# Four layers of graph convolution on one core: the relation passes with twice the slots, selection buffers and PSUM quads, and their dense step a turn later

## The chip, the cores and the metric

One Trainium2 chip, one of its cores. The metric is the device time of one launch in microseconds, median of several runs. The kernel before takes 6027.67 us.

## The reference

`x` has 5000 nodes of 128 features and there are 80000 edges, sorted by destination. Four layers follow one another, each `x = x + layer(relu(layernorm(x)))`: attention over edges, a weighted sum over edges, three averaging convolutions, and three relational convolutions. The last is what this change touches. Each of its convolutions is

```
seg  = dst * 8 + etype
agg  = segment_sum(x[src], seg)            # per node and relation
mean = agg / max(count, 1)
out  = einsum('nrd,rdo->no', mean, W) + x @ root + b
```

with widths 128 to 256, 256 to 256 and 256 to 128, and a relu after the first two.

## The kernel before, in words

**Order of the products.** The kernel multiplies before it gathers. For every node it makes the 8 products with the relations' matrices and stores them as 8 rows of a table in DRAM (`tab_l3a`, `tab_l3b`, `tab_l3c`, 40960 rows of 256, 256 and 128 floats). An edge then needs the one row of its source and its relation, divided by the edge count (`WGT`), and the sum over the edges of a node is the convolution. So there are three relation passes, numbered 5, 6 and 7 in the code (`sums(5, ...)` and so on), each with 80000 / 128 = 625 tiles of 128 edges. Pass 0, in an earlier layer, has the same form.

**A pass.** POOL gathers a tile by one indirect DMA (line 945, `gather`) into one of 16 slots of `ring`. Four tiles are a quad, and four quads, 16 tiles, are a turn; there are 157 quads and 39 turns. For each quad DVE makes a selection matrix in two instructions (lines 1776 and 1778, `select`): where an edge's destination falls in a window of 64 nodes, times the weight. PE multiplies each tile's rows by it and adds up the four tiles in a PSUM bank (line 2365, `tile`), and DVE adds the quad to the accumulator in SBUF at the window's place (line 1789, `quad`), one of `ACC_A` and `ACC_B`, features by nodes.

**What paces it.** Semaphores alone. `mm_done` counts quads that PE has finished: POOL waits for it before it refills the slots of the quad four before, DVE before it adds. `s_ready` counts selections, `psum_free` counts adds. DVE selects two quads ahead (`AHEAD`), in four buffers of `QSEL`; PE uses PSUM banks 0 to 3, one quad each, and may write a quad when the one four before has been added. The credits are at lines 2360 and 2361:

```
pe.wait_ge(sem("s_ready"), kr * (QUADS + AHEAD) + g + 1)
pe.wait_ge(sem("psum_free"), kq + g + 1)
```

**The dense step.** Beside pass 5 the table of pass 6 is made and beside pass 6 that of pass 7, a block of 128 nodes in each turn. The function `turns` says which block's steps stand in which turn and `dense_step` puts the 16 steps between the 16 tiles: tiles 0 to 3 of turn i carry the last four steps of block i - 2, tiles 4 to 15 the first twelve of block i - 1. There are 40 blocks, and two whole ones are left after the last turn (`remaining`). Step 0: ACT waits for the quad just added and makes the relu of the block's columns (line 1306, `hidden`) into `part_hid`, two buffers. Step 2: PE waits for it and multiplies by the root matrix (line 2396) into bank 5. Step 3: ACT adds the bias and stores it to the other accumulator, where the next pass starts (line 1102). Steps 4, 7, 10, 13: PE makes a unit, 512 columns of the block's table rows (line 2406), in banks 6 and 7 by turns; pass 6 has steps 4 and 7 alone. Two steps after each, ACT copies the bank to `unit_rows` (line 1112), and PE waits for the copy before it writes this bank again. SP stores a block's rows to the table (line 836, `store_units`). Pass 7 has no table to make: ACT copies a block (line 1330), PE transposes it into bank 4 or 5 (line 2669), DVE adds `x` (line 2217) and SP stores the result (line 855).

**Between passes.** POOL starts the gathers of a pass when the table is stored, DVE when all root products are in the accumulator.

## Time and profile before

| what | value |
|---|---|
| median of 3 runs | 6027.67 us (6023.32 to 6033.74) |
| profiled execution, first to last instruction | 6607.7 us |
| its own time beside the span | not given by the page; at least the span |
| PE, DVE, ACT, POOL busy in it | 4440, 2724, 1078, 4114 us |
| mean granted TensorE clock | 0.718 of full |
| relation passes | 3784.7 to the end |

The profile is one execution while every instruction is recorded. Its times are microseconds from its first instruction. Engines are PE (TensorE), PEld (its weight loads), DVE (VectorE), ACT (ScalarE), POOL (GpSimd) and SP. An fp32 matmul stands as two records. In a row of waits the engine and line are the ones that waited; "issue" is a time in which nothing that the profile knows held the engine, "remote" one that ended by a signal for which it found no recorded work that had just ended.

### The profile page before, as it was taken

The numbers are of one execution on the slowest core, as the hardware profiler recorded it, in microseconds if no ns is written. First come the engines' busy times: TensorE is split into PE (matmuls) and PEld (weight loads), VectorE is DVE, ScalarE is ACT, GpSimd is POOL, SyncE is SP. The second block draws the span as 40 slices with busy tenths as digits, with TensorE's granted clock in tenths as the row PEclk, the third lists the DMA queues.
The fourth block names the chain that finished last, engine by engine and source line by source line (L and its number), as shares of the span: only waits on it lengthen the run. The fifth ranks groups of instructions, "written<-read, shape, count | busy, mean of one in ns | idle before, by whom it ended". The sixth has DMA issues, their size and how long they took to land.

```text
span 6607.7 us, 91944 instructions
## 1 busy us (share of the span) xinstructions
PE 4440.1 (67%) x24058; PEld 3442.2 (52%) x24058; DVE 2723.9 (41%) x8965; ACT 1077.6 (16%) x2081; POOL 4113.5 (62%) x3656
## 2 busy tenths in 40 slices
PE   2456676666666665999989977777766776533333
PEld 1344555544444444988876655555555555433333
DVE  7965555677777774322236411111111111111112
ACT  2521111122222222111113311111100000000000
POOL 2356666488888885744445466666566666566666
PEclk6566666666666666999999977888867666655555
DMA  6622222256555555744457734444333333211111
GB/s 158 210 71 77 76 77 76 67 100 102 99 98 100 99 100 153 221 146 131 125 177 255 255 121 132 133 130 133 122 109 114 110 111 109 75 52 50 52 50 50
DMA packets 569636, 764.26 MB, mean 116 GB/s; under 512 B 87625, under 2 KB 468064, under 8 KB 558608
## 3 DMA queue, kind: packets, MB, share of 16 engines
q1 hardware_dynamic: 327884, 422.38, 20.1%
q0 software_dynamic: 190256, 287.00, 20.1%
q10 hardware_dynamic: 51334, 52.94, 2.4%
q8 instruction: 75, 1.23, 0.1%
q14 instruction: 87, 0.71, 0.0%
HBM read 526.51 MB, written 235.79 MB: 115 GB/s over the span
## 4 chain that ended last, share of the span: by engine, by line
PE 32%; issue 17%; another core or an unknown queue 16%; DVE 11%; DMA 10%; POOL 9%; DVEq 3%; ACT 1%; ACTq 0%; POOLq 0%; SPq 0%
PE PS L2495 10%; DMA part<-ring,cur 8%; PE PS L2365 7%; POOL ring L945 5%; PE PS L2406 5%; POOL part L967 3%; DVE ACC_B L1755 2%; PE PS L2632 2%; PE PS L2396 2%; PE PS L2330 1%; DVE ACC_B L1753 1%; DVE QSEL L1776 1%; PE PS L2427 1%; PE PS L2572 1%
## 5 line engine op out<-in xcount | busy, mean ns | idle before, releaser
L2365 PE MATMUL PS<-QSEL,ring 128*128 128x64 f32 x7436 | 1393.7, 339 | 723.0 <-issue 327.9
L2365 PEld LDWEIGHTS PS<-QSEL,ring 128*128 128x128 f32 x7436 | 1354.3, 257 | 937.1 <-issue 671.3
L967 POOL DMA_INDIRECT part<-ring,cur x625 | 1010.0, 1616 | 250.9 <-issue 154.3
L945 POOL DMA_INDIRECT ring<-tab_l3b,SRC x625 | 599.7, 959 | 357.5 <-issue 208.6
L945 POOL DMA_INDIRECT ring<-tab_l3a,SRC x625 | 596.7, 955 | 359.0 <-issue 197.8
L945 POOL DMA_INDIRECT ring<-tab_l,SRC x593 | 587.9, 991 | 360.7 <-issue 160.8
L945 POOL DMA_INDIRECT ring<-tab_l3c,SRC x625 | 598.4, 957 | 326.0 <-issue 202.4
L2330 PE MATMUL PS<-ACC_B 128*128 128x320 f16 x2568 | 622.5, 410 | 116.2 <-issue 60.7
L1789 DVE TENSOR_TENSOR ACC_B<-ACC_B,PS 128x128 f32 (+1 forms) x314 | 79.7, 254 | 1429.1 <-remote 1006.6
L2406 PE MATMUL PS<-XM,SCR 128*128 128x512 f32 x960 | 580.7, 737 | 28.6 <-issue 14.5
L2427 PE MATMUL PS<-SCR,SEL 128*32 128x128 f32 x1250 | 275.2, 402 | 418.4 <-DVE SCR L1825 334.8
L1755 DVE TENSOR_SCALAR ACC_B<-ACC_B 128x640 f16<-128x640 f16 x1284 | 498.4, 450 | 0.0
L2330 PEld LDWEIGHTS PS<-ACC_B 128*128 128x128 f16 x2568 | 300.1, 127 | 359.0 <-issue 118.1
L2427 PEld LDWEIGHTS PS<-SCR,SEL 128*32 128x32 f32 x1250 | 188.7, 160 | 482.4 <-DVE SCR L1825 355.6
L1753 DVE TENSOR_SCALAR ACC_B<-ACC_B 128x128 f16<-128x128 f16 x1284 | 253.1, 287 | 339.2 <-PE PS L2330 257.9
L1789 DVE TENSOR_TENSOR ACC_A<-ACC_A,PS 128x64 f32 (+1 forms) x314 | 78.7, 251 | 726.7 <-remote 498.2
L1059 ACT CAST ACC_B<-PS 128x640 f16<-128x640 f32 x320 | 221.5, 692 | 586.7 <-PE PS L2330 334.0
L1112 ACT COPY SCR<-PS 128x512 f32<-128x512 f32 x240 | 138.2, 587 | 1095.8 <-remote 652.7
L2406 PEld LDWEIGHTS PS<-XM,SCR 128*128 128x128 f32 x960 | 204.1, 235 | 199.9 <-issue 182.2
L2040 DVE TENSOR_TENSOR SCR<-PS,ring 128x128 f32<-128x128 f32 (+1 forms) x120 | 40.2, 335 | 586.6 <-PE PS L2495 571.2
L2495 PE MATMUL PS<-ACC_exact,slots_exact 128*128 128x512 f32 x1070 | 263.8, 397 | 0.0
L1776 DVE TENSOR_TENSOR QSEL<-iotaQ,QREL 128x256 f32<-128x256 f32 x477 | 201.5, 422 | 87.2 <-issue 86.2
(494 smaller groups left out, 6767.0 us busy)
## 6 DMA issues: line engine op xcount, KB each, us to landing
ring<-pairs_d SPq DMA_DIRECT2D x60, 1280.0 KB
pairs_d<-ACC_B ACTq DMA_DIRECT2D x320, 160.0 KB
SCR<-pairs_d SPq DMA_DIRECT2D x40, 1280.0 KB
SCR<-in_src SPq DMA_DIRECT2D x128, 320.0 KB
tab_l3a<-SCR SPq DMA_DIRECT2D x40, 1024.0 KB, 4.4
tab_l3b<-SCR SPq DMA_DIRECT2D x40, 1024.0 KB
ACC_A<-pairs_d SPq DMA_DIRECT2D x20, 1280.0 KB
tab_l3c<-SCR SPq DMA_DIRECT2D x40, 512.0 KB
```

What stands on the lines that cost most here:

```text
L945: pool.indirect_dma_start(gathered(p, slot), None, tab[p][:, :], bass.IndirectOffsetOnAxis(SRC[:, t:t + 1], 0)).then_inc(sem(f"pair_in{slo ...
L967: pool.indirect_dma_start(part_d[m][:, :], bass.IndirectOffsetOnAxis(cur[:, s:s + 1], 0), ring[:, s, 0:D], None, compute_op=ALU.add).then_ ...
L1059: nc.scalar.copy(SPAN_OUT[:, v, :].rearrange("p (h c) -> p h c", h=2), PS[:, 6:8, 0:SPAN_COLS // 2]).then_inc(sem("span_out"), 1)
L1753: vec.tensor_scalar(LOWS[:, v, e, :], iota_low, LOW[:, bass.ds(tile + e, 1)], None, ALU.is_equal)
L1755: ins = vec.tensor_scalar(PAIRS[:, v, e, :], iota_pairs, KEY[:, bass.ds(tile + e, 1)], OFFS[:, bass.ds(at, 1)], ALU.subtract, ALU.is_equal)
L1776: vec.tensor_tensor(hot[:, s, :, :], there, at, ALU.is_equal).then_inc(sem("s_hot"), 1)
L1789: vec.tensor_tensor(v, v, PS[:, s, 0:C * QWIN].rearrange("p (c w) -> p c w", w=QWIN), ALU.add).then_inc(sem("psum_free"), 1)
L2330: ins = mm(PS[:, 6 + h, 0:SPAN_COLS // 2], LOWS[:, v, e, :], PAIRS[:, v, e, h * (SPAN_COLS // 2):(h + 1) * (SPAN_COLS // 2)], start=e == 0 ...
L2365: ins = mm(PS[:, s, ch * QWIN:(ch + 1) * QWIN], rows, hot, start=e == 0 and ch == 0, stop=e == end, skip_group_check=True)
L2406: ins = mm(PS[:, 6 + m % 2, :], part_hid[:, u, ch, :], relw[:, at:at + 512], start=ch == 0, stop=ch == kc - 1)
L2427: ins = mm(windows_out[0:WIN, j * P:(j + 1) * P], SEL[:, j, :], same[:, j, :], start=True, stop=True)
L2495: ins = mm(to if conv == 1 else to.rearrange("p (k n) -> p k n", k=2), slot[:, e * P:(e + 1) * P], conv_source(conv, h), start=h == 0, sto ...
```

## The change

- The three relation passes leave `turns`, `remaining` and `sums` for functions of their own (`deep_turns`, `deep_remaining`, `deep_sums`, and `deep_steps` on ACT). Pass 0 keeps the old ones, now cut to its case.
- The gather has 32 slots (`DEEP`): the 16 of `ring` and 16 in `MULTI`, a buffer that is free by then. POOL waits for the quad eight before, and a landing semaphore counts a quad, not a pair.
- Selections have 8 buffers (`SEL_BUFS`), four of them in `MULTI`, made in place, and DVE selects 6 quads ahead (`LEAD`).
- PSUM banks 0 to 3 hold two quads each. PE waits once for every pair of quads, and DVE waits for both before it adds the first.
- The dense step of a block stands one turn later (`DEEP_LAG`: tiles 0 to 3 carry block i - 3, tiles 4 to 15 block i - 2), so three whole blocks are left after the last turn. Its relu is made by DVE in the middle of the turn, after the first pair's adds, block i - 1 in turn i; PE uses it at tile 6 of turn i + 1. DVE waits there for the copies of the block two before.
- Units stand at steps 3, 5, 7 and 11 in banks 6, 7, 4 and 6, ACT's copies one step later, and one semaphore counts them.

The diff, cut to its core:

```diff
+DEEP = 2 * SLOTS
+SEL_BUFS = 8
+LEAD = 6
+DEEP_LAG = 3
...
+        def deep_turns(eng, turn):
+
+            turn(0, None, None, 0, 0)
+            turn(1, None, None, 1, 0)
+            turn(2, None, (0, 0, 0), 0, 1)
+            pairs = (TURNS - DEEP_LAG) // 2 - 1
+            with eng.Fori(0, pairs) as r:
+                turn(2 * r + DEEP_LAG, (2 * r, 0, r), (2 * r + 1, 1, r), 1, r + 1)
+                turn(2 * r + DEEP_LAG + 1, (2 * r + 1, 1, r), (2 * r + 2, 0, r + 1), 0, r + 2)
+            for b in range(2 * pairs, TURNS - DEEP_LAG):
+                turn(b + DEEP_LAG, (b, b % 2, b // 2), (b + 1, (b + 1) % 2, (b + 1) // 2), (b + DEEP_LAG) % 2, (b + DEEP_LAG) // 2)
...
-            return ring_flat[:, slot * D:(slot + 1) * D] if p == 0 else ring[:, slot, 0:PASS[p]["F"]]
+            if p == 0:
+                return ring_flat[:, slot * D:(slot + 1) * D]
+            if slot < SLOTS:
+                return ring[:, slot, 0:PASS[p]["F"]]
+            return MULTI[:, (slot - SLOTS) * HID:(slot - SLOTS) * HID + PASS[p]["F"]]
+
+        def chosen_by(s):
+
+            if s < 4:
+                return QSEL[:, s, :, :]
+            at = SLOTS * HID + (s - 4) * QUAD * QWIN
+            return MULTI[:, at:at + QUAD * QWIN].rearrange("p (e w) -> p e w", e=QUAD)
+
+        def deep_landings(quad):
+
+            return sum(t % DEEP // QUAD == quad for t in range(T))
+
+        def deep_sums_bank(s):
+
+            return s % SEL_BUFS // 2, s % 2 * HID
 
...
+        UNIT_BANK = (6, 7, 4, 6)
+        UNIT_STEPS = (3, 5, 7, 11)
...
-                slots, per = (FIRST_SLOTS, QUAD) if p == 0 else (SLOTS, 2)
+                slots, per = (FIRST_SLOTS, QUAD) if p == 0 else (DEEP, QUAD)
...
-            def hidden(p, acc, k, b, u, added):
-                act.wait_ge(sem("psum_free"), added)
-                nc.scalar.activation(part_hid[:, u, :, :], block_cols2(acc, b), ACT.Relu).then_inc(sem("hid_made"), 1)
-
             def t6_dense(j, k, b, u, r, added):
-                if j == 0:
-                    hidden(6, ACC_B, k, b, u, added)
                 if j == 3:
                     root_bias(ACC_A, 3, 2, nth_block(act, km, k, b, 0), b)
-                if j in (6, 9, 12, 15):
-                    unit_rows_out(6, (j - 6) // 3, k, b, u, r)
-            dense_steps(5, t6_dense)
+                if j - 1 in UNIT_STEPS:
+                    unit_rows_out(6, UNIT_STEPS.index(j - 1), k, b, u, r)
+            deep_steps(5, t6_dense)
...
+            def deep_sums(p, hidden, dense):
+                c = PASS[p]
+                acc, C = c["acc"], chunks(p)
+                rounds_reset(f"p{p}")
+                with dve.Fori(0, km) as k:
+                    kq = dve.snap((km * ORD[p] + k) * QUADS)
+                    hots = dve.snap(km * (QUADS + AHEAD) + (km * (ORD[p] - 1) + k) * QUADS)
+                    round_start(f"p{p}", k)
+                    if hidden is not None:
+                        dve.wait_ge(sem("unit_out"), nth_block(dve, km, k, 0, p - 5, TABLES[p + 1][1], 4) + 1)
+
+                    def select(g, s):
+                        if isinstance(g, int) and g >= QUADS:
+                            return
+                        there = iotaQ[:, :].unsqueeze(1).to_broadcast([P, QUAD, QWIN])
+                        at = cols(QREL, g, QUAD).unsqueeze(2).to_broadcast([P, QUAD, QWIN])
+                        hot = chosen_by(s % SEL_BUFS)
+                        vec.tensor_tensor(hot, there, at, ALU.is_equal).then_inc(sem("s_hot"), 1)
+                        dve.wait_ge(sem("s_hot"), hots + g + 1)
+                        vec.tensor_tensor(hot, hot, cols(c["wt"], g, QUAD).unsqueeze(2).to_broadcast([P, QUAD, QWIN]), ALU.mult) \
+                            .then_inc(sem("s_ready"), 1)
+
+                    def quad(g, s, first):
+                        bank, at = deep_sums_bank(s)
+                        dve.wait_ge(sem("psum_free"), kq + g + CREDIT)
+                        v = acc[:, 0:C, bass.ds(first, QWIN)]
+                        vec.tensor_tensor(v, v, PS[:, bank, at:at + C * QWIN].rearrange("p (c w) -> p c w", w=QWIN), ALU.add).then_inc(sem("psum_free"), 1)
+
+                    def pair(g, s, bases):
+                        select(g + LEAD, s + LEAD)
+                        dve.wait_ge(sem("mm_done"), kq + g + 3)
+                        quad(g, s, bases[0])
+                        select(g + LEAD + 1, s + LEAD + 1)
+                        quad(g + 1, s + 1, bases[1])
+
+                    def block_hidden(b, u, added):
+                        dve.wait_ge(sem("psum_free"), added)
+                        if not isinstance(b, int) or b >= 2:
+                            dve.wait_ge(sem("unit_out"), nth_block(dve, km, k, b, p - 5, TABLES[p + 1][1], 4) - TABLES[p + 1][1] + 1)
+                        vec.tensor_scalar(part_hid[:, u, :, :], block_cols2(acc, b), 0.0, None, ALU.max).then_inc(sem("hid_made"), 1)
+
+                    def turn(i, last, first, h, use):
+                        bases = windows(dve, regs[0:4], QBASE[0:1, bass.ds(4 * i, 4)], QWIN)
+                        for x in range(2):
+                            g = 4 * i + 2 * x
+                            pair(g, 4 * h + 2 * x, bases[2 * x:2 * x + 2])
+                            if hidden is not None and x == 0 and later(i):
+                                block_hidden(i - 1, 1 - h, dve.snap(kq + g + 2 + CREDIT))
+                            for j in range(8 * x, 8 * x + 8):
+                                dense_step(dense, j, k, last, first, None)
+                    for g in range(LEAD):
+                        select(g, g)
+                    deep_turns(dve, turn)
+                    bases = windows(dve, regs[0:4], QBASE[0:1, bass.ds(QUADS - 1, 4)], QWIN)
+                    dve.wait_ge(sem("mm_done"), kq + QUADS + 1)
+                    quad(QUADS - 1, (QUADS - 1) % SEL_BUFS, bases[0])
+                    added = dve.snap(kq + QUADS + CREDIT)
+                    dve.wait_ge(sem("psum_free"), added)
+                    dve.sem_inc(sem("turn"), 1)
+                    if hidden is not None:
+                        for b in range(TURNS - 1, BLOCKS):
+                            block_hidden(b, b % 2, added)
...
+            def deep_sums(p, dense):
+                C = chunks(p)
+                with pe.Fori(0, km) as k:
+                    kr = pe.snap(km * (ORD[p] - 1) + k)
+                    kq = pe.snap((km * ORD[p] + k) * QUADS)
+                    chosen_before = pe.snap(km * (QUADS + AHEAD) + kr * QUADS)
+                    pe.wait_ge(sem("psum_free"), kq + CREDIT)
+                    pe.sem_inc(sem("turn"), 1)
+
+                    def landed(quad, use):
+                        return km * (16 * first_landings(quad)) + kr * (16 * deep_landings(quad)) + use * (16 * QUAD) + 16 * QUAD
+
+                    def tile(g, s, e, slot, landed, end):
+                        bank, at = deep_sums_bank(s)
+                        if e == 0:
+                            pe.wait_ge(sem(f"pair_in{slot // QUAD}"), landed)
+                            pe.wait_ge(sem("s_ready"), chosen_before + g + 1)
+                            if s % 2 == 0 and (not isinstance(g, int) or g >= SEL_BUFS):
+                                pe.wait_ge(sem("psum_free"), kq + g + (CREDIT + 2 - SEL_BUFS))
+                        rows, hot = gathered(p, slot), chosen_by(s)[:, e, :]
+                        for ch in range(C):
+                            ins = mm(PS[:, bank, at + ch * QWIN:at + (ch + 1) * QWIN], rows[:, ch * P:(ch + 1) * P], hot,
+                                     start=e == 0 and ch == 0, stop=e == end, skip_group_check=True)
+                        if e == end:
+                            ins.then_inc(sem("mm_done"), 1)
+
+                    def turn(i, last, first, h, use):
+                        for j in range(TURN):
+                            slot = h * TURN + j
+                            tile(4 * i + j // QUAD, 4 * h + j // QUAD, j % QUAD, slot, landed(slot // QUAD, use) if j % QUAD == 0 else None, QUAD - 1)
+                            dense_step(dense, j, k, last, first, None)
+                    deep_turns(pe, turn)
+                    last = (T - 1) % DEEP
+                    tile(QUADS - 1, (QUADS - 1) % SEL_BUFS, 0, last, landed(last // QUAD, (T - 1) // DEEP) - 16 * (QUAD - 1), 0)
+                    deep_remaining(lambda j, b, u, r: dense(j, k, b, u, r, None))
...
-                emptied = nth_block(pe, km, k, b, p - 6, units // 2, 2)
-                pe.wait_ge(sem("unit_outd" if m % 2 else "unit_outa"), emptied + m // 2 + 1)
+                pe.wait_ge(sem("unit_out"), nth_block(pe, km, k, b, p - 6, units, 4) + (2 if m == 3 else 1))
                 for ch in range(kc):
                     at = (ch * units + m) * 512
-                    ins = mm(PS[:, 6 + m % 2, :], part_hid[:, u, ch, :], relw[:, at:at + 512], start=ch == 0, stop=ch == kc - 1)
+                    ins = mm(PS[:, UNIT_BANK[m], :], part_hid[:, u, ch, :], relw[:, at:at + 512], start=ch == 0, stop=ch == kc - 1)
...
-                if j in (4, 7, 10, 13):
-                    unit(6, (j - 4) // 3, k, b, u)
-            sums(5, t6_dense)
+                if j in UNIT_STEPS:
+                    unit(6, UNIT_STEPS.index(j), k, b, u)
+            deep_sums(5, t6_dense)
```

## Rows read from the trace of the kernel before

**Rows 1.** The page's first line: the profiled execution.
```profile
span 6607.7 us, 91944 instructions
```

**Rows 2.** Line 945, the gathers: ns min/median/max, first and last start in us.
```profile
L945 POOL DMA_INDIRECT ring<-tab_l3a,SRC x625: 943/949/1167, 3784.7 to 4714.8; - x157
L945 POOL DMA_INDIRECT ring<-tab_l3b,SRC x625: 943/949/1196, 4751.0 to 5672.0; - x157
L945 POOL DMA_INDIRECT ring<-tab_l3c,SRC x625: 942/947/1202, 5695.8 to 6596.3; - x157
```

**Rows 3.** Same view: POOL idle before gathers of all four passes: us, times.
```profile
  remote: 495.6, 174
  PE PS L2365: 82.2, 56
  PE PS L2367: 55.8, 14
```

**Rows 4.** POOL's waits in each relation pass: waited for, us, times, longest.
```profile
POOL ring L945 <- remote: 109.0, 39, 4.0
POOL ring L945 <- PE PS L2365: 52.2, 29, 4.3
...
POOL ring L945 <- remote: 120.2, 36, 4.6
POOL ring L945 <- PE PS L2365: 28.8, 23, 4.3
...
POOL ring L945 <- remote: 122.4, 37, 5.9
POOL ring L945 <- PE PS L2365: 1.2, 4, 0.3
```

**Rows 5.** Third relation pass, timeline: start us, us, what, idle before and its releaser.
```profile
6129.51 1.12 PE L2365 MATMUL PS<-QSEL,ring 128*128 128x64 f32 x4 [1.19 <-DMA ring<-tab_l3c,SRC]
...
6134.52 1.12 PE L2365 MATMUL PS<-QSEL,ring 128*128 128x64 f32 x4 [1.25 <-DMA ring<-tab_l3c,SRC]
...
6136.89 0.95 POOL L945 DMA_INDIRECT ring<-tab_l3c,SRC  x1 [0.31 <-issue]
...
6141.49 0.22 DVE L1789 TENSOR_TENSOR ACC_B<-ACC_B,PS 128x64 f32 x1 [16.45 <-remote]
6141.63 0.42 DVE L1776 TENSOR_TENSOR QSEL<-iotaQ,QREL 128x256 f32<-128x256 f32 x1
6142.07 0.95 POOL L945 DMA_INDIRECT ring<-tab_l3c,SRC  x1 [4.24 <-remote]
...
6142.52 0.22 DVE L1789 TENSOR_TENSOR ACC_B<-ACC_B,PS 128x64 f32 x1
```

**Rows 6.** POOL's waits in the scatter stretch, 1300 to 2500: the largest.
```profile
POOL part L967 <- issue: 149.7, 483, 0.6
```

**Rows 7.** Stretches: busy us of PE, PEld, DVE, ACT, POOL; PE clock, DMA, GB/s.
```profile
3784.00:4715.00 931.00, 721.76 (x3367) 524.06 (x3368) 161.33 (x459) 122.26 (x260) 595.97 (x625) 0.80 0.42 131
4751.00:5672.00 921.00, 636.06 (x2917) 517.41 (x2918) 160.95 (x462) 73.18 (x150) 598.73 (x625) 0.68 0.36 110
5695.00:6597.00 902.00, 332.93 (x1282) 287.74 (x1282) 163.57 (x496) 11.31 (x38) 598.08 (x625) 0.50 0.19 51
4715.00:4751.00 36.00, 26.22 (x95) 13.79 (x93) 6.47 (x20) 9.44 (x20) 0.77 (x1) 0.97 0.33 112
```

**Rows 8.** Timeline of the tails of the first and second relation pass.
```profile
4726.51 0.42 ACT L1306 ACTIVATE SCR<-ACC_B 128x256 f32<-128x256 f32 x1
...
4726.98 1.16 PE L2396 MATMUL PS<-SCR,root 128*128 128x128 f32 x8 [0.99 <-ACT SCR L1306]
...
4735.52 0.42 ACT L1306 ACTIVATE SCR<-ACC_B 128x256 f32<-128x256 f32 x1
...
5681.41 0.42 ACT L1306 ACTIVATE SCR<-ACC_A 128x256 f32<-128x256 f32 x1 [3.42 <-DVE ACC_A L1789]
...
5686.54 0.42 ACT L1306 ACTIVATE SCR<-ACC_A 128x256 f32<-128x256 f32 x1
```

More of the change, by code:

```diff
@@ L431, in dense_step, with deep_remaining @@
                 dense(j - SLACK, k, *first, added)
+        def deep_turns(eng, turn):
[8 more added lines that the diff above has]
+                turn(b + DEEP_LAG, (b, b % 2, b // 2), (b + 1, (b + 1) % 2, (b + 1) // 2), (b + DEEP_LAG) % 2, (b + DEEP_LAG) // 2)
+        def deep_remaining(step):
+            for b in range(TURNS - DEEP_LAG, BLOCKS):
+                for j in range(TURN - SLACK if b == TURNS - DEEP_LAG else 0, TURN):
+                    step(j, b, b % 2, b // 2)
         def remaining(step):
@@ L1083, in dense_steps, with deep_steps @@
                     remaining(lambda j, b, u, r: dense(j, k, b, u, r, added))
+            def deep_steps(p, dense):
+                with act.Fori(0, km) as k:
+                    kq = act.snap((km * ORD[p] + k) * QUADS)
+                    def turn(i, last, first, h, use):
+                        added = act.snap(kq + TURN // QUAD * (i - 1) + (CREDIT + SLACK // QUAD)) if first is not None else None
+                        for j in range(TURN):
+                            dense_step(dense, j, k, last, first, added)
+                    deep_turns(act, turn)
+                    added = act.snap(kq + QUADS + CREDIT)
+                    deep_remaining(lambda j, b, u, r: dense(j, k, b, u, r, added))
             def norm_root(n):
@@ L2373, in turn @@
                         for j in range(TURN):
-                            slot = u * TURN + j if p == 0 else j
-                            tile(4 * i + j // QUAD, j // QUAD, j % QUAD, slot, None if p == 0 and last is None else landed(slot, i if p else r), QUAD - 1,
-                                 TURN * i + j if p == 0 and last is None else None)
+                            slot = u * TURN + j
+                            tile(4 * i + j // QUAD, j // QUAD, j % QUAD, slot, None if last is None else landed(slot, r), QUAD - 1,
+                                 TURN * i + j if last is None else None)
                             dense_step(dense, j, k, last, first, added)
@@ L2387, in sums, with turn @@
                     added = pe.snap(kq + QUADS + CREDIT)
                     remaining(lambda j, b, u, r: dense(j, k, b, u, r, added))
+            def deep_sums(p, dense):
[11 more added lines that the diff above has]
+                        if e == 0:
+                            pe.wait_ge(sem(f"pair_in{slot // QUAD}"), landed)
+                            pe.wait_ge(sem("s_ready"), chosen_before + g + 1)
[7 more added lines that the diff above has]
+                            ins.then_inc(sem("mm_done"), 1)
+                    def turn(i, last, first, h, use):
+                        for j in range(TURN):
+                            slot = h * TURN + j
[4 more added lines that the diff above has]
+                    tile(QUADS - 1, (QUADS - 1) % SEL_BUFS, 0, last, landed(last // QUAD, (T - 1) // DEEP) - 16 * (QUAD - 1), 0)
+                    deep_remaining(lambda j, b, u, r: dense(j, k, b, u, r, None))
```

55 lines of the change are left out of this document (22 added, 33 removed).

## The prediction, made before the change was run

> **What bounds the kernel now.** I read the profile from the outside in: the span, the gathers of the three relation passes, what their engine waited for, one held stretch, PE's clock, and what follows a pass's last gather. The profiled execution spans 6607.7 us [rows 1]; the median of the runs is 6027.7, that is 580.0 less. This gap carries much of the forecast and comes back below.
>
> The relation passes take 625 gathers each, one after another on POOL: first start to last start 930.1, 920.9 and 900.6 us [rows 2]. A gather is busy for 0.95 us and the next follows 0.30 later [rows 5], so 625 that never wait need 625 x 1.25 = 781 us. The rest is waiting for a free slot: 109.0 + 52.2 = 161.2 us in the first of the passes, 120.2 + 28.8 = 149.0 in the second, 122.4 + 1.2 = 123.6 in the third, 433.8 together [rows 4]. Over all four gather passes the kinds of wait sum to 495.6 + 82.2 + 55.8 = 633.6 us [rows 3]. No other engine bounds them: PE is busy 721.8 of 931 us, 636.1 of 921 and 332.9 of 902, DVE 161 to 164 [rows 7].
>
> What releases these waits is PE's signal that a quad is done, and it comes late. In [rows 5] PE ends one quad at 6129.51 + 1.12 = 6130.63 and the next at 6135.64, 5.0 us apart. DVE, which needs only the signals, begins the adds of waiting quads at 6141.49 and 6142.52, 1.0 us apart, after 16.45 us of idleness that no recorded release explains ("remote"). POOL stopped after the gather of 6136.89 and went on at 6142.07, 4.24 us idle. The third pass has 37 such waits, longest 5.9 us [rows 4]: about one for each time that POOL goes round its 16 slots. In the scatter stretch, where POOL's largest wait is mere issue [rows 6], that view has no remote entry at all. So a signal held for up to 16 us meets a ring of 16 slots, which is 16 x 1.25 = 20 us deep, of which landing and PE's work already take a part.
>
> **The change part by part.** (a) *32 slots instead of 16.* A quad's slots are wanted again after eight quads, 40 us, not after four, 20 us. No gather is added. If a held signal comes through chiefly once POOL has gone quiet ([rows 5]: 3.6 us after POOL's last busy moment, 6136.89 + 0.95), the same pause of some 4 us is paid once per 32 gathers: the stall halves. If it comes through on its own in 16 us, the 40 us hide it and the stall goes. If it lasts as long as the ring, or is not a delay of the signal at all, nothing goes. I take the half: the pauses recur at the ring's period and the release seen came only in the quiet. Ends: nothing and all.
>
> (b) *Eight selection buffers, lead of six; eight quads in PSUM.* Before, PE may run two quads past what DVE has been told; it stops for s_ready or psum_free, which is why a deeper ring alone would be useless. The two selection instructions per quad (0.42 us each [rows 5]) are only issued earlier; DVE has 930 - 161 us of room. At a pass's start four more quads are selected ahead, 4 x 0.84 = 3.4 us, beside the first gathers' landing; only the first selection is awaited. Cost nothing. DVE adds quads in pairs, so every other add waits up to one quad (5 us), which the eight buffers cover; if they did not, PE would stop and (a) would be lost.
>
> (c) *Dense step a turn later, relu on DVE.* 40 relus in each of two passes leave ACT (0.42 us each [rows 8]) and stand in DVE's queue, between the adds; the nearest DVE instruction, the selection of the same 128x256, takes 0.42 too. 80 x 0.42 = 34 us on DVE, hidden by its idleness. Bounds: 0, or 34 if each stood before an add that POOL awaits; I take 0. DVE now also waits there for the copies of the block two before: queued behind it are the second half of the turn's adds and selections, but those copies precede the quads just added in PE's order. In exchange PE's root product at tile 6 no longer waits for a relu of the same turn.
>
> (d) *Three unit banks.* Unit products and their copies are as many as before, 160 and 80. The waits for a freed bank go from 6 tiles' distance to 8 (bank 6) or 16 (7 and 4). Bank 4 held the transposes of the last pass only, which still has it. SP's wait is merged, its stores are as many, POOL's landing semaphore now covers four gathers: PE starts a quad up to 2.5 us later, inside the 40. Nothing on the path; if PE did not have the room, see the third rival.
>
> (e) *The tail.* Blocks left after a pass's last quad: three whole ones instead of two. A block in the first tail takes 4735.52 - 4726.51 = 9.0 us, in the second 5686.54 - 5681.41 = 5.1 [rows 8]; in each, 0.99 us is PE idle for the relu, which DVE now makes ahead. First tail: +9.0 - 3 x 1 = +6; second: +5.1 - 3 = +2; in the last pass, a copy and a transposition more, +1. Together +9 us, all on the path, for POOL may not start the next pass before the table is stored. Bounds: 0, and 9.0 + 5.1 + 1 = 15.
>
> **The sum.** Against the profiled execution: -433.8 / 2 + 9 = -208, so a span near 6400. For the runs I need the share of the stall that they have. The stall of all gather passes, 633.6, is a little more than the whole excess of the profiled execution, 580.0. If all of the excess is stall that recording brings about, the runs keep 53.6 of 633.6, 8%, and the three passes have 37 us of it. If none is, they keep it all, scaled by 6027.7 / 6607.7 = 0.912: 396 us. No row divides the excess (91944 recorded instructions may each cost a little too), so I take half of it: 633.6 - 290 = 343.6, 54%, and 433.8 x 0.54 = 235 us in the three passes. Half of that goes: -118 + 9 = -109, and 6027.7 - 109 = 5919.
>
> **Rivals.** *1, nothing to be had.* Either the runs hardly stall: -18 + 9 = -9, 6018; or the hold lasts until POOL stops, and the pauses grow with the ring: +9, 6037. For it: how nearly 580 and 633.6 agree. Against: the waits are much alike in all three passes, whatever PE's load. Here stands also that PE is truly as late as its signals and its records stand too early. Against that, [rows 5]: DVE finds two quads done 1.0 us apart, of which each took PE two bursts of 1.1 us. The Trainium skill, "Perfetto Trace Analysis", section "Tensor Engine Instruction (MATMUL, LD_WEIGHTS)", says that a matmul's recorded end is estimated and that its semaphore is pushed only after PSUM has acknowledged. By that rule PE would be the true bound, a deeper ring would bring nothing, and the time would be 6037; DVE's starts disagree with it, at least in size.
>
> *2, the ring hides it all.* The hold is a delay of some 16 us and 40 us of slots cover it: -235 + 9 = -226, 5802; with all the stall in the runs -396 + 9, 5641. For it: DVE's idle of 16.45 us [rows 5] is well under 40. Against: the signal came only when POOL was quiet.
>
> *3, slower: PE in the first relation pass.* PE did 721.8 us of work at a granted clock of 0.80 [rows 7], 577 at full clock. It lies between the levels of 1.2 and 2.4 GHz; in the last pass, busy 333 of 902 us, it was 0.50, and in the first tail, nearly without gaps, 0.97. A hold that lasts 40 us leaves PE waiting for unit banks, then with eight quads and two blocks to make up at the low level. Below a mean clock of 577 / 931 = 0.62 PE becomes the bound of this pass. At 0.56, midway to the floor: 577 / 0.56 = 1031, +100, +91 in the runs; with +9 and half of the other two passes' stall, 272.6 x 0.54 / 2 = 74, gained: 6054. The second pass has 636.1 x 0.68 = 433 and could not become PE-bound above 0.47. Against it: the lead of six lets PE work through a hold that stops it today. The Trainium skill, "TensorE: Matmul & The Clock Gate", section "Why this matters for your kernels", warns that idle gaps between bursts send the clock back to its lower level; [rows 7] agree (0.50 with gaps, 0.97 without).
>
> **How the numbers follow.** A measurement of this kernel can tell 0.2%, 12 us, from no change. Forecast 0.40, rival 1 0.20, rival 2 0.22, rival 3 0.15, others 0.03. Faster: 0.40 + 0.22 and a little of rival 1, 0.66. Same 0.17, slower 0.17. The time is that of the likeliest, 5919. The range runs from 5720, between rival 2 and its extreme, to 6060, past rival 3: left out are a full hiding of a full stall and a PE slower than 0.56. The forecast's own range, from a quarter to three quarters of the excess, is 5870 to 5970.
>
> **What would show it.** Right: POOL's waits in the three passes about 217 us in place of 433.8, half as many; passes of some 850, 845 and 840 us; PE busy at a clock no lower than 0.75 in the first; relus on DVE at 0.4 us; the gap to the next pass 6 us longer. (a) is wrong if as many waits remain or each is twice as long; (b) if PE waits for selections; (d) if PE waits for unit copies; (e) if the tails do not grow. The split of the excess is wrong if the changed kernel's span falls by 200 and its runs by under 30, or by as much as the span. The forecast fails if the span falls by less than 100.

## The result, and the profile after

The changed kernel takes 6040.46 us, median of 11 runs (6039.15 to 6046.54). The kernel before, run beside it, takes 6029.61 (11 runs, 6023.32 to 6036.15). The ratio is 1.002, with a 95% interval of 1.0012 to 1.0028: slower by 0.2%, 10.9 us. The forecast was 5919.

The first view is the head of the changed kernel's page and its gathers, each pass now in two rows, one for the 16 slots in `ring` and one for the 16 in `MULTI` (`XM` in the trace). The columns are those of [rows 2].

```profile
span 6038.5 us, 91019 instructions
...
L985 POOL DMA_INDIRECT ring<-tab_l3a,SRC x320: 942/947/1194, 3601.3 to 4390.8; - x160
L985 POOL DMA_INDIRECT XM<-tab_l3a,SRC x305: 942/947/1182, 3621.8 to 4392.0; - x153
...
L985 POOL DMA_INDIRECT ring<-tab_l3b,SRC x320: 941/947/1192, 4431.4 to 5217.0; - x160
L985 POOL DMA_INDIRECT XM<-tab_l3b,SRC x305: 942/947/1193, 4451.8 to 5218.3; - x153
...
L985 POOL DMA_INDIRECT ring<-tab_l3c,SRC x320: 940/945/1199, 5240.4 to 6026.2; - x160
L985 POOL DMA_INDIRECT XM<-tab_l3c,SRC x305: 940/945/1187, 5260.3 to 6027.4; - x153
```

The passes, first start to last start, are 790.7, 786.9 and 787.1 us, against 930.1, 920.9 and 900.6 in [rows 2]. That looks like a gain of 387 us, yet the time did not fall. Note the span: 6038.5 here against 6607.7 in [rows 1], while the runs of the two kernels are 11 us apart. The two profiled executions are not alike in something other than the kernel. POOL's waits in the first and the second pass, as in [rows 4]:

```profile
POOL ring L985 <- issue: 120.3, 315, 24.6
POOL XM L985 <- issue: 91.1, 299, 0.3
POOL XM L985 <- PE PS L2516: 1.8, 6, 0.3
POOL ring L985 <- PE PS L2516: 1.5, 5, 0.3
...
POOL ring L985 <- issue: 133.2, 312, 38.4
POOL XM L985 <- issue: 90.8, 298, 0.3
POOL ring L985 <- PE PS L2516: 2.4, 8, 0.3
POOL XM L985 <- PE PS L2516: 2.1, 7, 0.3
```

What is left is the 0.30 us between one gather and the next. The waits put down to PE sum to 3.3 and 4.5 us, none of them longer than 0.3, and the third pass has none. Engines and clock by stretch, with the columns of [rows 7]:

```profile
3600.00:4393.00 793.00, 663.51 (x3349) 501.86 (x3350) 169.22 (x496) 108.34 (x219) 601.48 (x625) 0.84 0.48 153
4393.00:4431.00 38.00, 31.44 (x112) 16.93 (x110) 7.62 (x23) 10.68 (x21) 0.00 (x0) 0.97 0.35 126
4431.00:5219.00 788.00, 627.14 (x2914) 515.73 (x2915) 171.01 (x492) 56.43 (x110) 597.42 (x625) 0.68 0.43 129
...
5240.00:6029.00 789.00, 308.45 (x1278) 280.08 (x1278) 157.46 (x490) 11.01 (x37) 597.84 (x625) 0.50 0.22 58
```

Nothing of rival 3: PE's clock in the first pass is 0.84, and it works 31 of 38 us in the tail. So there were two questions: what does the kernel *before* look like in an execution like those that were timed, and where do 11 us come from?

### The profile page after: what moved, and what is told of

It reads as the page before. It is cut to its first block, busy times and chain, and to the rows that moved or that the text cites. A ratio compares the mean times of both kernels' runs of the same rounds, so it can differ in the third digit from the quotient of the medians.

```text
span 6038.5 us, 91019 instructions
## 1 busy us (share of the span) xinstructions
PE 4329.7 (72%) x24058; PEld 3381.9 (56%) x24058; DVE 2738.3 (45%) x9033; ACT 1049.6 (17%) x2001; POOL 4110.3 (68%) x3656
## 3 DMA queue, kind: packets, MB, share of 16 engines
q0 software_dynamic: 190256, 287.00, 22.1%
## 4 chain that ended last, share of the span: by engine, by line
POOL 38%; PE 23%; issue 16%; DMA 14%; DVE 6%; DVEq 1%; ACT 1%; POOLq 1%; SPq 0%; ACTq 0%
POOL ring L985 21%; POOL XM L985 13%; DMA part<-ring,cur 11%; PE PS L2635 11%; POOL part L1007 3%; PE PS L2516 2%; PE PS L2772 2%; PE PS L2546 2%; PE PS L2441 1%; PE PS L2712 1%; PE PS L2714 1%; PE PS L2725 1%; DVE ACC_B L1801 1%; DMA XM<-tab_l3b,SRC 0%; PE PS L2662 0%
## 5 line engine op out<-in xcount | busy, mean ns | idle before, releaser
L2516 PE MATMUL PS<-QSEL,ring 128*128 128x64 f32 x3200 | 570.1, 344 | 415.0 <-DMA ring<-tab_l3c,SRC 251.5
L2516 PEld LDWEIGHTS PS<-QSEL,ring 128*128 128x128 f32 x3200 | 549.4, 258 | 504.1 <-issue 463.5
L2516 PE MATMUL PS<-XM 128*128 128x64 f32 x3050 | 543.8, 344 | 372.4 <-DMA XM<-tab_l3c,SRC 229.8
L2516 PEld LDWEIGHTS PS<-XM 128*128 128x128 f32 x3050 | 523.8, 258 | 457.8 <-issue 419.3
L985 POOL DMA_INDIRECT ring<-tab_l3b,SRC x320 | 305.9, 956 | 135.6 <-issue 133.2
L985 POOL DMA_INDIRECT ring<-tab_l3a,SRC x320 | 308.2, 963 | 121.9 <-issue 120.3
L985 POOL DMA_INDIRECT ring<-tab_l3c,SRC x320 | 305.7, 955 | 118.4 <-issue 118.4
L985 POOL DMA_INDIRECT XM<-tab_l3a,SRC x305 | 293.3, 962 | 93.0 <-issue 91.1
L985 POOL DMA_INDIRECT XM<-tab_l3c,SRC x305 | 292.2, 958 | 93.0 <-issue 93.0
L985 POOL DMA_INDIRECT XM<-tab_l3b,SRC x305 | 291.7, 956 | 93.0 <-issue 90.8
L2473 PE MATMUL PS<-QSEL,ring 128*128 128x64 f32 x1186 | 261.2, 355 | 83.1 <-DMA ring<-tab_l,SRC 82.3
L2473 PEld LDWEIGHTS PS<-QSEL,ring 128*128 128x128 f32 x1186 | 245.7, 261 | 133.6 <-issue 118.5
```

The source lines that it names most:

```text
L985: pool.indirect_dma_start(gathered(p, slot), None, tab[p][:, :], bass.IndirectOffsetOnAxis(SRC[:, t:t + 1], 0)).then_inc(sem(f"pair_in{slo ...
L2473: ins = mm(PS[:, s, ch * QWIN:(ch + 1) * QWIN], rows, hot, start=e == 0 and ch == 0, stop=e == end, skip_group_check=True)
L2516: ins = mm(PS[:, bank, at + ch * QWIN:at + (ch + 1) * QWIN], rows[:, ch * P:(ch + 1) * P], hot, start=e == 0 and ch == 0, stop=e == end, s ...
```

## The experiments

Each table row below is one kernel: its time (median, lowest to highest, runs), the kernel before on the same chip, and the ratio with its interval. The stages come from one profile each: first to last gather of the three relation passes, then the two gaps (last gather of a pass to first of the next) and the end (last gather to the end of the span).

### The kernel before again, and 16 slots

`before_again` is the kernel before, unchanged. 

> The kernel before, unchanged, profiled once more. Theory T (tail): the late signals of PE belong to the first profiled execution and not to the kernel; here the span is within 10 us of the 6029.6 us of its runs, each relation pass takes 785 to 800 us from first to last gather, POOL's waits other than issue are under 30 us in all three passes, and the gap from the last gather of one pass to the first of the next is 31 to 37 and 18 to 24 us. Rival S (stall): the kernel before really stalls and the change gave the gain back elsewhere; here the passes take 840 us or more and POOL waits 40 us or more in each.

Its gathers, and POOL's waits put down to PE in the three passes:

```profile
L945 POOL DMA_INDIRECT ring<-tab_l3a,SRC x625: 942/946/1197, 3597.9 to 4384.0; - x157
...
L945 POOL DMA_INDIRECT ring<-tab_l3b,SRC x625: 942/946/1197, 4417.4 to 5207.2; - x157
...
L945 POOL DMA_INDIRECT ring<-tab_l3c,SRC x625: 940/944/1163, 5231.6 to 6014.3; - x157
```

```profile
POOL ring L945 <- PE PS L2365: 16.7, 55, 0.3
...
POOL ring L945 <- PE PS L2365: 9.1, 30, 0.3
...
POOL ring L945 <- PE PS L2365: 19.5, 64, 0.3
```

This settles the larger question. The same kernel, recorded in the same way, now spans 6022.2 us and takes 6023.9, so recording costs nothing that is seen here. With 16 slots its passes are 786.1, 789.8 and 782.8 us: as short as with 32. No wait is longer than 0.3 us, which is the usual distance between two gathers under another name. There is no stall to remove.

`slots16` is the changed kernel with its ring put back to 16 slots, all else kept:

```diff
-DEEP = 2 * SLOTS
+DEEP = SLOTS
...
-                            slot = h * TURN + j
-                            tile(4 * i + j // QUAD, 4 * h + j // QUAD, j % QUAD, slot, landed(slot // QUAD, use) if j % QUAD == 0 else None, QUAD - 1)
+                            slot = j
+                            tile(4 * i + j // QUAD, 4 * h + j // QUAD, j % QUAD, slot, landed(slot // QUAD, 2 * use + h) if j % QUAD == 0 else None, QUAD - 1)
```

> The changed kernel with 16 slots again, all else of it kept (selection lead, eight quads in PSUM, late dense step, relu on DVE, banks). Theory T: POOL has nothing to wait for with 16 slots either, so 6040 us, within 6 of the changed kernel. Rival S: the ring is what keeps POOL going, so the passes lengthen by 40 us each and the time is above 6100.

### The tail: a lag of two turns, and the changed kernel again

`lag2` keeps the ring, the buffers, the banks and the relu on DVE, but moves the dense step a turn forward again. The root product then stands at tile 6 of the turn in which the relu is made, and the units at 7, 8, 10 and 14.

```diff
-DEEP_LAG = 3
+DEEP_LAG = 2
...
-        UNIT_STEPS = (3, 5, 7, 11)
+        UNIT_STEPS = (7, 8, 10, 14)
...
```

> The changed kernel with the dense step as early as before (two whole blocks left after the last quad, not three), its root product and units at later tiles of the turn because DVE makes the relu after a pair of quads. Theory T: the third block is what the change added to the path, 7.8 us in the first tail, about 4 in the second and 1 in the last: 6040.5 - 13 = 6027, at or a little under the kernel before. Rival S: the tail is not what costs; the time stays at 6040 or rises, because PE again waits for the relu of the same turn.

`after_again` is the changed kernel once more, for a second profile. 

> The changed kernel, unchanged, profiled once more, to see whether late signals of PE turn up in a profile of it. Theory T: a span within 10 us of 6040 as in its first profile, no such signals; if they do turn up, they are a matter of the execution. Rival S: the same, so this run tells only of how far one profile can be trusted.

| kernel (chip 0; before 6029.33, 21 runs) | time | ratio | passes | gaps, end |
|---|---|---|---|---|
| before_again | 6023.92, one | | 786.1, 789.8, 782.8 | 33.4, 24.4, 7.9 |
| slots16 | 6041.23 (6031.92 to 6043.96, 11) | 1.002 [1.0011, 1.0029] | 786.6, 785.8, 784.1 | 40.5, 25.0, 11.0 |
| lag2 | 6037.51 (6034.58 to 6043.75, 11) | 1.0017 [1.0008, 1.0026] | 788.4, 787.8, 787.7 | 35.1, 25.4, 8.9 |
| after_again | 6034.17, one | | 787.5, 785.6, 784.1 | 39.6, 22.4, 11.1 |

Going back to 16 slots changes neither time nor passes: the ring is worth nothing here, and costs nothing. The gaps and the end sum to 65.7 us in the kernel before, to 72.6 in the first profile of the changed one (39.4 + 22.1 + 11.1) and to 73.1 in the second. `lag2` brings the sum to 69.4, but was expected at 6027 and came to 6037.5: 3 us of the 13 hoped for. The end of its first pass, and the first product of a whole block after it:

```profile
4388.70 0.95 POOL L984 DMA_INDIRECT XM<-tab_l3a,SRC  x1 [0.30 <-issue]
4390.07 0.58 ACT L1165 COPY SCR<-PS 128x512 f32<-128x512 f32 x1 [1.54 <-PE PS L2545]
...
4401.07 1.16 PE L2536 MATMUL PS<-SCR,root 128*128 128x128 f32 x8
4401.20 0.58 ACT L1165 COPY SCR<-PS 128x512 f32<-128x512 f32 x1 [2.02 <-PE PS L2545]
```

Four copies of an earlier block's units, from 4390.07 to 4401.20, stand behind the last gather, and the first root product of a whole block comes 12.4 us after it. The changed kernel has four such copies too, but its root product follows after 8.8 (4400.84 - 4392.03 in its first profile). From that product to the first gather of the next pass `lag2` takes 22.7 us and the changed kernel 30.6. So the third block costs the 7.8 us that were expected of it, and 3.6 of them are lost again in the stretch before the whole blocks. That the later steps of `lag2` do this is likely but not shown, as this stretch varies by itself: it is 11.7 us in `after_third`. Its second gap, 25.4, is longer than the changed kernel's 22.1.

### One part each, on a chip that behaves like the first profile

The next four ran on another chip. `before_third` is the kernel before. 

> The kernel before, unchanged, profiled a third time. Theory T: as in its second profile, span 6015 to 6035, passes of 783 to 790 us, gaps of about 33.4 and 24.4 us, 8 us at the end, first relation gather near 3598 us (if it is nearer 3602, as in both profiles of the changed kernel, the part ahead of the relation passes adds nothing to the difference). Rival R (rare state): a span above 6500 with late signals of PE again.

`late_only` is the kernel before with the dense step of passes 5 to 7 a turn later and nothing else: the order of turns and of what remains is that of the change, and ACT's relu awaits the adds of the turn before.

```diff
...
-                        added = act.snap(kq + TURN // QUAD * i + (CREDIT + SLACK // QUAD))
+                        added = act.snap(kq + TURN // QUAD * (i if p == 0 else max(i - 1, 0) if isinstance(i, int) else i - 1) + (CREDIT + SLACK // QUAD))
...
-                    turns(act, turn)
+                    (late_turns if p else turns)(act, turn)
```

> The kernel before with one part of the change, the dense step a turn later in the three relation passes; relu on ScalarE, 16 slots, two unit banks as before. Theory T: a whole block more in each tail at the price of before, 9.0 and 5.1 us and 1 to 3 at the end: gaps of 42 and 29.5 us, 6029.3 + 16 = 6045 us, slower than the changed kernel, whose relu made ahead gives part of it back. Rival P (the passes): the tail is paid for by fewer waits inside the passes and the time stays at 6029.

`lead2` is the changed kernel with DVE selecting two quads ahead, as before, in place of six.

```diff
-LEAD = 6
+LEAD = 2
```

> The changed kernel with selections made 2 quads ahead instead of 6. Theory T: POOL is never held by PE, so the lead is worth nothing, 6040 us within 6, or 1 to 3 us less at each pass start, where fewer selections are made first. Rival P: the lead keeps PE from stopping, and without it the passes lengthen and the time rises above 6050.

`relu_ahead` is the kernel before with nothing changed but the relu, made by DVE after the turn's first quad.

```diff
-                if j == 0:
-                    hidden(6, ACC_B, k, b, u, added)
...
+                            if relu and g == 0 and first is not None:
+                                block_hidden(first[0], first[1], added)
```

> The kernel before with one other part of the change, the relu on VectorE, here right after the turn's first quad; dense step no later, 16 slots, two unit banks. Theory T: in the tails PE no longer waits 0.99 us for the second block's relu and little less for the first: gaps 1 to 2 us shorter each, 6029.3 - 3 = 6026 us, which may not be told from before. Rival P: VectorE's relu holds up its adds, POOL waits, and the time rises to 6035 or more.

| kernel (chip 7; before 6577.69, 23 runs) | time | ratio | passes | gaps, end |
|---|---|---|---|---|
| before_third | 6579.0, one | | 922.7, 913.3, 893.0 | 33.9, 26.9, 11.2 |
| late_only | 6584.64 (6571.57 to 6595.8, 11) | 1.001 [1.0002, 1.0019] | 919.5, 911.3, 893.1 | 42.3, 28.2, 10.0 |
| lead2 | 6607.81 (6591.65 to 6613.46, 6) | 1.0041 [1.0029, 1.0053] | 917.0, 913.3, 891.7 | 60.1, 32.5, 19.1 |
| relu_ahead | 6578.26 (6568.92 to 6580.9, 11) | 1 [0.9991, 1.0009] | 922.0, 913.9, 894.3 | 35.1, 26.7, 8.7 |

On this chip the kernel before takes 6578 us, all 23 runs, recorded or not, where it takes 6029 on chip 0. POOL's waits in the first and the second pass of `before_third` are those of [rows 4]:

```profile
POOL ring L945 <- remote: 100.7, 38, 3.8
POOL ring L945 <- PE PS L2365: 48.8, 24, 4.3
...
POOL ring L945 <- remote: 132.5, 37, 4.2
POOL ring L945 <- PE PS L2365: 11.7, 25, 4.4
```

So the excess of 580 us in the profile that the prediction was read from is that of such a chip, not of recording (its span is still 30 us longer than the one here, which stays open), and the runs of 6027.67 were taken on one like chip 0. What can be held against the expectations is each kernel's distance from its own kernel before. The later dense step costs 7 us here, of the 16 expected, and shows in the first gap (33.9 to 42.3). The relu on DVE is worth nothing either way. `lead2` is the costliest, and its cost stands after the last gathers, in gaps of 60.1 and 32.5 and an end of 19.1: PE has work left when POOL has none. Most of that belongs to the changed kernel and not to its shorter lead: on a like chip, below, the changed kernel has gaps of 58.2 and 32.7 and an end of 16.2. There it is 13.2 us above its kernel before, `lead2` is 30.1 above here. Compared across the two chips, the lead of six is worth some 17 us where signals are late; the expectation had nothing.

### The same parts on a clean chip

The four were repeated, with the changed kernel in place of the kernel before, on a third chip.

`after_third`: 

> The changed kernel unchanged, beside the kernel before. The earlier calls met two chips: on one the kernel before runs in 6029 us and its profile has no late signal of PE, on the other in 6578 us with signals up to 17 us late, as in the profile that the prediction was made from. Theory C (a property of the chip): if this call meets the second chip, both kernels are near 6580 and late signals stand in this profile too. There theory H (the pause per 32 gathers) expects the passes shorter by 60 to 80 us each and 6370 us; theory L (the signals come only when POOL stops, the hold grows with the ring) expects passes of 910 to 925 as before and, PE being further behind at the end of a pass, 6590 to 6610. On the first chip: 6040 and 6029.

`late_again`: 

> The kernel before with the dense step a turn later only. On the first chip theory T expects 6029 + 16 = 6045 us and gaps of 42 and 29.5; rival P 6029. On the second, as measured there, 0.1% above the kernel before.

`lead2_again`: 

> The changed kernel with selections 2 quads ahead. On the first chip theory T expects 6040 us within 6, like the changed kernel, with passes of 784 to 791 us; rival P passes above 800. On the second, as measured there, 0.4% above the kernel before; if the changed kernel in this call is faster than that, the lead of six is worth the difference where signals are late.

`relu_again`: 

> The kernel before with the relu on VectorE only. On the first chip theory T expects 6026 us, gaps of about 31.5 and 23 us, not to be told from before by its time; rival P 6035 or more. On the second, as measured there, the time of the kernel before.

| kernel (chip 3; before 6027.91, 30 runs) | time | ratio | passes | gaps, end |
|---|---|---|---|---|
| after_third | 6035.64 (6027.06 to 6045.19, 10) | 1.0016 [1.0006, 1.0026] | 788.1, 785.4, 785.0 | 42.2, 21.3, 11.0 |
| late_again | 6043.4 (6037.73 to 6052.27, 9) | 1.0028 [1.0018, 1.0038] | 786.2, 788.0, 783.3 | 43.0, 28.6, 9.9 |
| lead2_again | 6037.74 (6027.86 to 6043.59, 10) | 1.0016 [1.0007, 1.0026] | 790.3, 785.9, 784.6 | 39.7, 22.6, 11.1 |
| relu_again | 6028.19 (6025.09 to 6034.38, 10) | 1.0002 [0.9993, 1.0012] | 789.9, 788.3, 782.1 | 35.8, 22.9, 7.9 |

The later dense step alone costs 15.5 us (6043.4 - 6027.9), more than the whole change: +9.6, +4.2 and +2.0 in the gaps and the end against `before_again` (on chip 0), 15.8 together. The other parts give back 7.8 of it (to 6035.64), in the second gap above all (28.6 to 21.3). Here the lead of six is worth nothing (6037.7 against 6035.6), and the relu on DVE by itself nothing (6028.2 against 6027.9).

### The change where PE is held up

Was the changed kernel's short first profile the work of its ring, or of its chip? One more pair ran on a fourth chip. `after_fourth` is the changed kernel, `slots16_again` is `slots16`.

> The changed kernel unchanged, in search of the chip on which PE's signals are late. There theory H (a pause per 32 gathers, so half the stall) expects relation passes 60 to 80 us shorter each than the kernel before has there (922.7, 913.3, 893.0) and about 6370 us; theory L (a held signal comes only when POOL stops, and what PE is behind is made up after the pass) expects passes of 890 to 925, longer gaps after them (over 45 us after the first) and 6560 to 6610. On a chip without late signals: 6036 to 6041 beside 6028 to 6030.

> The changed kernel with 16 slots, on the same chip. Where signals are late, theory H expects it near the kernel before, some 200 us above the changed kernel, since the ring is what halves the pauses; theory L expects it within 20 us of the changed kernel. Where they are not late: 6041 as before, within 6 of the changed kernel.

| kernel (chip 12; before 6579.08, 19 runs) | time | ratio | passes | gaps, end |
|---|---|---|---|---|
| after_fourth | 6592.28 (6589.66 to 6602.15, 10) | 1.002 [1.0011, 1.003] | 922.4, 914.0, 885.6 | 58.2, 32.7, 16.2 |
| slots16_again | 6581.08 (6576.13 to 6590.69, 10) | 1.0001 [0.9991, 1.001] | 920.7, 913.7, 891.8 | 42.4, 28.4, 13.3 |

This chip behaves like chip 7, and the changed kernel is as slow on it: 6592 us. So 32 slots don't take the stall away where there is one. POOL's waits in the third pass of `after_fourth`, and in the last line DVE's longest:

```profile
POOL XM L985 <- remote: 61.0, 14, 8.7
POOL ring L985 <- remote: 34.3, 10, 6.4
POOL ring L985 <- PE PS L2516: 3.7, 1, 3.7
POOL XM L985 <- PE PS L2516: 3.1, 1, 3.1
...
DVE ACC_B L1888 <- remote: 526.3, 31, 35.1
```

The same of `before_third`, DVE alone:

```profile
DVE ACC_B L1789 <- remote: 451.2, 44, 17.5
```

The third pass has 26 waits where [rows 4] have 41. But `before_third` has 29 there, and both average 3.9 us (102.1 and 113.1 in all); only the longest grew, from 5.9 to 8.7. The total of the three passes is 387.8 us in 144 waits, against 406.8 in 153 in `before_third` (149.5 + 144.2 + 113.1) and 397.3 in 163 in `slots16_again`: 5% less, not half, and 2.7 us a wait as in `before_third`. DVE's longest wait in the third pass is 17.5 us in `before_third`, 23.9 in `slots16_again` and 35.1 here, so part of its growth comes with the ring. And what POOL gains as a head start comes back after the pass. From `slots16_again` to `after_fourth` the gaps and the end grow by 23.0 (84.1 to 107.1), the passes shrink by 4.2, and the first pass starts 7.4 earlier: 11.4, which is the difference of the two spans (11.5) and of the two times (11.2).

## Why the prediction was wrong

**The size of the stall in the runs** is the step that failed: the term of 235 us, of which half was to go. The sum took 54% of the recorded stall for the runs, 235 us in three passes, because no row divided the excess of 580 us between stall and recording. It had put 0.40 on that. The right share is none: `before_again` has 625 gathers in 786, 790 and 783 us, and 625 x 1.25 = 781 was in the text. Rival 1 had this case, "the runs hardly stall", at 6018, with 37 us left to halve. That nothing was to be had was right; 37 was still too much, as these waits are the ordinary 0.3 us each. Its cause was wrong too: it took the excess for "stall that recording brings about", and it is one of the chip.

There was a row to see it by, and I gave it too little weight. The stall (633.6) and the excess (580.0) agreed within a tenth. Of explanations that put the stall in the runs too, none made these two agree. I counted that for rival 1 and took a half all the same, between two ends that I could not rank.

**(a), half of the stall.** Wrong as well, by itself. The forecast was half as many waits, each as long as before. On the chips that have the stall each is as long (2.7 us), but as many remain, which was the text's own sign against (a): 58, 60 and 26 in the three passes of `after_fourth`, against 62, 62 and 29 in `before_third` and 68, 59 and 41 in [rows 4]. The whole change takes 5% of the stall (406.8 to 387.8), its ring about half of that (397.3 to 387.8), and loses that and more in the gaps. In its time rival 1's other half was nearer, a hold that lasts until POOL has stopped and pauses that grow with the ring: it had +9, and chip 12 shows +13.2. But the average pause did not grow, only the longest did, with DVE's longest wait. I had argued against it from waits "much alike in all three passes", which does not speak to it.

**(b), selections and PSUM.** Right on a clean chip: `lead2_again` equals the changed kernel, and in the changed kernel's first pass PE's matmuls wait 2.8 us for selections in all. Where signals are late the lead is worth some 17 us. **(c), relu on DVE at nothing.** Right: `relu_again` is at 1.0002. The price was too high besides. The relus take 0.29 us each, not 0.42. **(d), unit banks.** Right in that the waits of PE in the first two passes name no copy. Those of `before_again` name none either, and no run had the three banks alone, so what they are worth is not shown.

**(e), the tail.** Near in the sum, 9 us forecast, and it is the only part of the result that is explained. But the sum came out by luck, as its parts missed to both sides. By parts, +6, +2 and +1 were forecast. The three profiles of the changed kernel on clean chips show +6.0, +6.2 and +8.8 in the first gap, -2.3, -2.0 and -3.1 in the second, and +3.2, +3.2 and +3.1 at the end, or +6.9, +7.4 and +8.8 together. The tail of the first pass, in the timeline of the changed kernel:

```profile
4400.84 1.11 PE L2537 MATMUL PS<-SCR,root 128*128 128x128 f32 x8
...
4409.48 0.29 DVE L1901 TENSOR_SCALAR SCR<-ACC_B 128x256 f32<-128x256 f32 x1 [7.41 <-ACT SCR L1166]
4409.75 0.63 ACT L1156 ACTIVATE ACC_A<-PS,bcol 128x128 f32<-128x128 f32 x2 [0.30 <-PE PS L2537]
...
4417.56 0.63 ACT L1156 ACTIVATE ACC_A<-PS,bcol 128x128 f32<-128x128 f32 x2 [0.30 <-PE PS L2537]
...
4431.40 0.94 POOL L985 DMA_INDIRECT ring<-tab_l3b,SRC  x1 [38.42 <-issue]
```

In `relu_again`, the kernel before with the relu alone moved, the same two lines are these:

```profile
4408.33 0.62 ACT L1102 ACTIVATE ACC_A<-PS,bcol 128x128 f32<-128x128 f32 x2 [0.85 <-PE PS L2406]
...
4416.09 0.62 ACT L1102 ACTIVATE ACC_A<-PS,bcol 128x128 f32<-128x128 f32 x2 [0.30 <-PE PS L2406]
```

From one block's bias to the next is 4417.56 - 4409.75 = 7.81 us, where [rows 8] have 9.0: 1.2 less, for 1 us allowed. With the relu alone it is 7.76, so the relu made ahead accounts for it, and nothing is left for the unit banks. A gap has two stretches: from the last gather to the first root product of a whole block, and from there to the next pass's first gather. Read from the timelines, in us:

| profile | blocks | first gap | second gap |
|---|---|---|---|
| before_again | 2 | 9.4 + 24.0 | 7.7 + 16.7 |
| relu_again | 2, relu ahead | 13.1 + 22.8 | 10.3 + 12.6 |
| late_again | 3 | 9.9 + 33.1 | 6.6 + 22.1 |
| first profile of the change | 3, relu ahead | 8.8 + 30.6 | 4.7 + 17.4 |

The sum priced the second stretch, and rightly in the first tail: +6.5, for +6 forecast (the third block 9.0, less the relus). In the second tail it is +0.7 for +2, as the relu ahead saves 4.1 on two blocks there (16.7 to 12.6) and not 2. The first stretch it put at nothing. That stretch differs by some us from kernel to kernel, it is 3 us shorter in the second tail of the changed kernel, and it takes back from `relu_again` what its blocks gain. What sets it was not found, nor why the end grows by 3 and not by 1.

From 10.9 us in the runs the tail explains 7 to 9. The rest lies ahead of the passes or in them (the first gather stands at 3601 to 3602 in these profiles against 3597.9), and single profiles can't settle it: `relu_again`, whose time is that of the kernel before, begins them at 3604.2. Pass and gap also trade with one another: 790.7 + 39.4 in the first profile and 788.1 + 42.2 in `after_third` are 830.1 and 830.3. No version tried beats the kernel before; the relu alone equals it on both kinds of chip, and `slots16_again` does on chip 12.

The second half of the check that the text set, a span that falls by 200 with runs that fall by under 30, was not what came either: the span fell by 569 and the runs rose. Both spans were taken for those of one kind of chip, and they were not.

## What to carry to other kernels

When the profiled execution and the timed runs of one kernel are 10% apart, find out which of the two the stall belongs to before pricing its removal: a stall whose sum matches the excess is the excess until a row says otherwise. And a lag that buys slack inside a pass is paid at each place where the pipeline drains, whether or not the slack was needed.

## What the runs showed of the hardware

**Four chips, two times.** The kernel before takes 6029.3 and 6027.9 us on chips 0 and 3, and 6577.7 and 6579.1 on chips 7 and 12, with 19 to 30 runs on each, none in between. The scatter stretch takes 1204.5 us on chip 0 and 1210.8 on chip 7; the first gather pass takes 841.7 and 982.1. It is the stretches with gathers from a table that differ: the four gather passes hold 510.7 of the 555.1 us between the spans of `before_third` and `before_again`. Each chip was met on one occasion, so that the chip makes the difference, and not the occasion, is likely but not shown.

**On chips 7 and 12 PE or its signals come late while POOL gathers.** This is PE in the third pass of `after_fourth`, in a hold that ends with POOL's longest wait:

```profile
5757.19 0.26 PE L2516 MATMUL PS<-QSEL,ring 128*128 128x64 f32 x1 [2.52 <-issue]
5760.69 0.27 PE L2516 MATMUL PS<-QSEL,ring 128*128 128x64 f32 x1 [3.24 <-issue]
5762.79 0.26 PE L2516 MATMUL PS<-QSEL,ring 128*128 128x64 f32 x1 [1.84 <-issue]
5765.59 0.27 PE L2516 MATMUL PS<-QSEL,ring 128*128 128x64 f32 x1 [2.54 <-issue]
5767.69 0.26 PE L2516 MATMUL PS<-QSEL,ring 128*128 128x64 f32 x1 [1.84 <-issue]
5769.09 0.27 PE L2516 MATMUL PS<-QSEL,ring 128*128 128x64 f32 x1 [1.13 <-issue]
5769.79 0.47 PE L2516 MATMUL PS<-QSEL,ring 128*128 128x64 f32 x1 [0.44 <-issue]
...
5771.98 0.94 POOL L985 DMA_INDIRECT XM<-tab_l3c,SRC  x1 [8.71 <-remote]
```

And this is the same work in the first profile of the changed kernel:

```profile
5761.91 1.97 PE L2516 MATMUL PS<-XM 128*128 128x64 f32 x8 [3.08 <-DMA XM<-tab_l3c,SRC]
5766.92 1.97 PE L2516 MATMUL PS<-XM 128*128 128x64 f32 x8 [3.05 <-DMA XM<-tab_l3c,SRC]
```

A quad is eight records in 1.97 us there. Here single records stand 1.4 to 3.5 us apart, with nothing that the profile knows to wait for. They close up to 0.7 only from 5769.09 on, when POOL, whose last gather began at 5762.32, has been quiet for 5.8 us. Such idleness of PE's tile line put down to issue sums to 330.2 us in that pass, and to nothing in the third pass of the changed kernel on a clean chip. But it is no measure of the stall: in the same pass it is 17.0 us in `slots16_again`, on the same chip, and 24.3 in `before_third`, where POOL's waits are 115.5 and 113.1 us, more than the 102.1 here. There, as in [rows 5], the records of a quad mostly stand at their usual pace and only its signal comes late. In the profile that the prediction was read from, such idleness is 238.5 us in the second pass and 23.6 in the third. So part of what the prediction took for a held signal is PE itself at a crawl. The Trainium skill, "Perfetto Trace Analysis", section "Tensor Engine Instruction (MATMUL, LD_WEIGHTS)", says that a matmul's recorded end is estimated. On the clean chips these traces show no need to doubt the ends, as a quad's signal rises 0.01 us after its recorded end there. What holds PE up on two chips of four was not found, and no experiment here could take it away.
